# Grouped-query attention between two feed-forward layers: the matmuls for the row maxima take 128 contraction rows instead of 64, from a second, zero-padded copy of the keys

## The reference, cut to what matters

```python
x = x + 0.5 * ffn(layernorm(x), W_up, W_gate, W_down)
q, k, v = ...                                   # heads of width 16; k and v shared by 4 query heads
scores = einsum('bhqd,bhkd->bhqk', q, k) / sqrt(16)
scores = where(causal, -inf, scores)            # 256 x 256 for each of 16 x 16 (sequence, head)
x = x + softmax(scores) @ v
x = x + 0.5 * ffn(layernorm(x), W_up, W_gate, W_down)
```

## Time and profile before

| | us |
|---|---|
| median of 3 runs | 680.62 |
| lowest, highest | 678.63, 680.65 |
| span of the profiled execution (first to last instruction) | 676.7 |
| what lies around the span, if that execution took the median time | 3.9 |
| PE, DVE, ACT, POOL busy within the span | 612.5, 552.8, 361.8, 309.7 |

### The profile page before, as it was taken

The page is one execution under the profiler, slowest core; times in us unless marked ns, Lnnn a source line. Parts: engine busy times, 40 slices in busy tenths (PEclk is TensorE's granted clock), DMA queues, the critical chain, the costliest instruction groups (busy, mean ns, idle before and its releaser), DMA issues.

```text
span 676.7 us, 14252 instructions
## 1 busy us (share of the span) xinstructions
PE 612.5 (91%) x4276; PEld 339.8 (50%) x4276; DVE 552.8 (82%) x1964; ACT 361.8 (53%) x652; POOL 309.7 (46%) x288
## 2 busy tenths in 40 slices
PE   1768999999897899996999699998888999999998
PEld 1324555656465644543444345443444555555566
DVE  6999989899967869794888479795959999899964
ACT  3444444444443357673677557776775444444442
POOL 6876624343412236563474627473674344243400
PEclk9999999999998979997999989998999999999999
DMA  9411001110105131413050503131021231121201
GB/s 310 148 32 31 17 16 31 31 31 5 28 1 116 41 80 41 80 43 80 1 118 1 118 1 90 30 94 26 3 33 32 32 63 46 46 62 32 63 32 62
DMA packets 48342, 36.40 MB, mean 54 GB/s; under 512 B 33697, under 2 KB 44705, under 8 KB 47777
## 3 DMA queue, kind: packets, MB, share of 16 engines
q1 hardware_dynamic: 48288, 35.80, 22.9%
HBM read 18.22 MB, written 9.44 MB: 41 GB/s over the span
## 4 chain that ended last, share of the span: by engine, by line
PE 64%; DVE 16%; issue 7%; DMA 6%; ACT 3%; SPq 2%; POOL 1%; DVEq 1%; POOLq 0%; ACTq 0%
PE bank L1023 22%; PE bank L1035 12%; PE bank L1118 8%; PE bank L1145 7%; PE bank L1173 6%; DVE hl L740 5%; DMA k_st<-k_scratch 5%; PE bank L1182 4%; DVE hid L714 2%; DVE stats L645 2%; PE bank L1187 2%; PE bank L1196 1%; ACT silu L462 1%; ACT shared L539 1%; SPq L228 1%
## 5 line engine op out<-in xcount | busy, mean ns | idle before, releaser
L878 DVE CUSTOM_DVE_ANT_0 sm_out<-bank,mask 128x256 f16<-128x256 f32 (+1 forms) x512 | 157.7, 352 | 60.8 <-PE bank L1145 40.4
L462 ACT ACTIVATE silu<-bank,w_scale 128x512 f32<-128x512 f32 x128 | 87.8, 686 | 167.8 <-PE bank L1023 167.6
L539 ACT ACTIVATE shared<-bank,qk_scale 128x512 f32<-128x512 f32 x192 | 125.8, 682 | 65.1 <-PE bank L1173 63.6
L740 DVE TENSOR_TENSOR hl<-hid,hh 128x512 f16<-128x512 f32 x128 | 140.6, 1098 | 0.0
L1035 PE MATMUL bank<-wT_down,hh 128*128 128x256 f16 x512 | 118.8, 273 | 8.1 <-DVE hl L740 7.5
L1035 PE MATMUL bank<-wT_down,hl 128*128 128x256 f16 x512 | 118.7, 273 | 0.0
L714 DVE SCALAR_TENSOR_TENSOR hid<-silu,h_unit,bank 128x512 f32<-128x512 f32 x128 | 94.7, 740 | 28.2 <-ACT silu L462 24.8
L1023 PE MATMUL bank<-xh,wT_gate 128*128 128x512 f16 x256 | 98.1, 383 | 9.6 <-DVE hid L714 9.0
L1023 PE MATMUL bank<-xh,wT_up 128*128 128x512 f16 x256 | 98.3, 384 | 1.9 <-DVE xl L699 1.9
L1023 PE MATMUL bank<-xl,wT_up 128*128 128x512 f16 x256 | 98.3, 384 | 0.0
L1023 PE MATMUL bank<-xl,wT_gate 128*128 128x512 f16 x256 | 98.0, 383 | 0.0
(11 more groups left out here) (113 smaller groups left out, 831.3 us busy)
## 6 DMA issues: line engine op xcount, KB each, us to landing
q_st<-q_scratch SPq DMA_DIRECT2D x16, 512.0 KB, 5.8
q_scratch<-q_hl SPq DMA_DIRECT2D x8, 512.0 KB, 3.2
out_dram<-x SPq DMA_DIRECT2D x7, 512.0 KB, 2.9
x<-in_x_dram SPq DMA_DIRECT2D x1, 3072.0 KB, 15.1
k_st<-k_scratch SPq DMA_DIRECT2D x32, 64.0 KB, 6.1
x<-in_x_dram SPq DMA_DIRECT2D x2, 512.0 KB, 7.2
shared<-in_w_up_t_dram SPq DMA_DIRECT2D x2, 512.0 KB, 5.3
shared<-in_w_gate_t_dram SPq DMA_DIRECT2D x2, 512.0 KB, 7.6
```

Of the source, the lines that this page charges most:

```text
L462: act.activation(silu[:, e % 2, :], U[e % 2][:, :], ACT.Silu, scale=w_scale[:, 0:1]).then_inc(silu_ready, 1)
L539: act.activation(prob[:, place % 2, i, :], ST[(3 * place + i) % 2][:, :], ACT.Exp, scale=qk_scale[:, 4:5]).then_inc(exp_done, 1)
L740: dve.tensor_tensor(hl[:, par, e, :], hid[:, e % 4, :], hh[:, par, e, :], ALU.subtract).then_inc(hl_ready, 1)
L878: ins = dve.tensor_tensor_reduce(sm_out[:, i, cols], SM[i][:, cols], mask[:, S - size:S], 1.0, MASKED, ALU.add, ALU.max, rowmax[:, seq_par ...
```

## The change

The keys are stacked a second time, in `k_mx`, whose rows 64 to 127 are zero, and the matmuls for the maxima take all 128 rows of `q_st` and `k_mx`. The zero rows cancel whatever stands in rows 64 and 65 of `q_st`. Each read of a chunk has four DMAs of 64 KB more, each put ahead of one of the old four, and all ten are waited for. POOL clears the new rows once, early.

```diff
+        k_mx = sb("k_mx", [P, 2, G, TC], F16)
...
-        N_SCR, N_ST = 2, 6
+        N_SCR, N_ST = 2, 10
...
                     for twice in range(2):
                         rows = slice((2 * n + twice) * DH, (2 * n + twice + 1) * DH)
+                        sp.dma_start(k_mx[rows, par, :, :], k_scr[par, n]).then_inc(st_loaded[par], 16)
                         sp.dma_start(k_st[rows, par, :, :], k_scr[par, n]).then_inc(st_loaded[par], 16)
...
-            sp.wait_ge(const_ready, 3)
+            sp.wait_ge(const_ready, 4)
...
             pool.memset(q_st[64:P, :, :, :].bitcast(U32), 0).then_inc(const_ready, 1)
             pool.wait_ge(const_ready, 3)
+            pool.memset(k_mx[64:P, :, :, :].bitcast(U32), 0).then_inc(const_ready, 1)
+            pool.wait_ge(const_ready, 4)
...
-                                        q_st[0:4 * DH, par, HPG * g + j, rows:rows + P],
-                                        k_st[0:4 * DH, par, g, at:at + size],
+                                        q_st[:, par, HPG * g + j, rows:rows + P],
+                                        k_mx[:, par, g, at:at + size],
```

## The result

The kernel with the change takes 687.0 us, the median of 7 runs (683.68 to 691.93), against 680.62 us of 7 runs before (678.63 to 682.63). The ratio is 1.0092, with a 95% interval of 1.0051 to 1.0133, so it is slower by more than nothing. The forecast was 681 us, its range 672 to 689: that range holds the time. The forecast's own case, no difference that can be told (0.40, 677 to 685), didn't come; slower had been given 0.38.

The account below looks back on a forecast made before the run. PE was taken as the bound, losing 0.11 us per matmul-shape change, with DVE close behind and reads on the chain. 676.7 less 15.6 plus 9.9 (reads) plus 6.0 (clock) is 677.0; with 3.9 around it, 681 us, range 672 to 689.

Parts of the forecast that it names:

- PE's shape, passed by DVE: In the stretches between reads, removed 64/128-row changes at 0.11 us each, as far as DVE allows: 15.6 us saved.
- reads on the path, five of them: First read, three between loop ends and the last each land 1.5 us later: 7.5 us added.
- the second read: Wanted 11.1 us after its first issue, while the longer read takes 10.9: hidden, nothing added.
- DVE's stop at two loop ends: DVE loads code behind the read's packets; more data lengthens this 0 to 2 us, taken as 1.2 each, 2.4.
- the clock: Longer PE stops halve it after three reads, 1.5 us each, plus 0.75 each at first and last: 6.0 us.
- rival 1: DVE is no limit, so PE's whole saving counts, 22 us for 15.6: 674.5 us; chance 0.17.
- Rival 5: The extra transfers cost only 0.5 us a read: 675 us; chance 0.06.
- Rival 3: At both loop ends code packets wait behind the longer queue; DVE's stop grows 4 us, not 1.2: 688; chance 0.14.
- rival 7: Code packets get ahead of a read's second half; DVE's stop shrinks up to 7 us per loop end: 667; chance 0.03.
- rival 2: The clock stays up after the three reads, 4.5 us less than forecast: 676.5 us; chance 0.14.
- Rival 6: 128-row weight loads can't run ahead of matmuls on the same rows; 512 loads of 0.1 us exposed, tens slower; chance 0.01.
- POOL's clearing: POOL's early clearing of the new rows takes 1.7 us, hidden because POOL then idles 1.69 us.

Follow-up runs that it names:

- shape_only: The kernel before with the maxima's matmuls on 128 rows of its own stacks, no second copy and rows 64 and 65 not cancelled: 668.17 us, ratio 0.9784.
- before_again: The kernel before, unchanged, run and profiled a second time: 683.19 us, ratio 0.9996.
- narrow pair: narrow_before and narrow_shape: DVE's reductions cut to 16 columns of each head, with 64-row and 128-row maxima: 673.1 and 648.82 us.
- tiny_bytes: The changed kernel with the four new DMAs of each read cut to one eighth of their columns, all ten issues kept: 669.93 us, ratio 0.98.
- narrow_before: The kernel before with DVE's reductions cut to the first 16 columns of each head, maxima still on 64 rows: 673.1 us, ratio 0.9849.
- reads_only: The changed kernel reading and awaiting the second copy, but with the maxima still on 64 rows of k_st: 701.6 us, ratio 1.018.
- narrow_shape: The kernel before with DVE's reductions cut to 16 columns of each head and maxima on 128 rows, no second copy: 648.82 us, ratio 0.9511.
- filler: The changed kernel with twelve useless matmuls ahead of PE's wait at the three reads between loop ends: 681.58 us, ratio 0.9982 to the kernel before.

## Why the prediction was right and wrong

The sum by its own terms, beside what the profiles gave. The measured shape saving is the span of shape_only against before, 10.8 us, plus the 1.6 us of the first feed-forward; the other rows are after against shape_only. They sum to 4.3 us, and with those 1.6 to the 5.9 between the spans (682.6 less 676.7). These are single executions: against before_again's span (680.7) the first row would be some 4 us larger, and by the ratios the shape is 14.7 us and all the rest 21.0. The last row is what the other rows leave, the stretches between the reads.

| term | predicted, us | measured, us |
|---|---|---|
| PE's shape, passed by DVE | −15.6 | −12.4 |
| reads on the path, five of them | +7.5 | +12.0 |
| the second read | 0 | +2.2 |
| DVE's stop at two loop ends | +2.4 | −2.3 |
| the clock | +6.0 | +4.8 |
| sum | +0.3 | +4.3 |

**The shape.** Right in mechanism and price, and the 15.6 us lie within what the two profiles of before and the ratios allow (12.4 to 16.5): the spacing went from 0.32 to 0.22 us, and PE's busy time in a stretch with 25 changes fell by 2.8 us, 0.11 each. That DVE stops it halfway was right too (rival 1, DVE no limit, fell with the narrow pair), but I spread it wrongly. By stretch, shape_only against before, with what I took: between reads 0.7, 1.1 and 1.1 us (1.6 each), 236.9 to 271.4 3.0 (2.3), behind the loop ends 2.5 and 0.7 (2.2 each), the last 0.9 (3.0), the first none (1.1). These make about 10 (the second, the loop ends' and the last hold falls of the clock too); the rest of the 12.4 came at the loop ends' stops and inside the reads, where I had put nothing. The Trainium skill (TensorEngine Tiling (Array Packing), Key Properties) says that changing the tiling mode drains TensorE. The trace agrees in so far as a change costs 0.11 us, which is gone without it; the drain itself it doesn't show.

**A read's length.** The step "twenty per cent of 6.9 us" is mis-sized. I took the bytes as a share of the engines' busy time, and added 0.1 for the issues: 1.5. The rate over the whole read stays at 139 to 140 GB/s, so 20% more bytes take 20% of the read's 9.5 us, 1.9; with the rest it came to 2.2 on average against before, and to 2.4 against shape_only for the five (12.0 by 5). By tiny_bytes some 1.7 of the 2.2 is bytes and 0.5 the issues. Rival 5, transfers at 0.5 each, fell. That the trace's 139 GB/s "doesn't agree" with the ceiling of 435 GB/s that the prediction gives from the Trainium skill (DMA: Bandwidth & Descriptors, Specifications) was too strong: a rate below a ceiling agrees with it, and shows only that the ceiling isn't what sets this read.

**The second read.** This is the step that failed: "Of eight reads the second is hidden". I set 10.9 us of read against 11.1 us of cover, as if the cover stood still. The cover is PE's own work from the trigger to the first use. The windows of before and of after over it:

```profile
236.90:248.00 11.10, 11.10 (x70) 5.30 (x69) 6.91 (x48) 6.13 (x12) 2.97 (x6) 0.69 0.60 121
```

```profile
240.70:249.00 8.30, 7.69 (x69) 4.26 (x68) 6.68 (x46) 5.95 (x12) 2.96 (x5) 1.00 0.91 173
```

The same work is 11.1 us long at a granted clock of 0.69 and 8.3 us at 1.00. So the cover was in part the slow clock, which I hadn't looked up for this stretch, and in part the changes of matmul. The narrow pair parts the two, with a light DVE and the clock at 1.00 in both: the cover is 7.8 us with 64 rows and 6.9 with 128. So the changes are some 0.9 us of it (I counted 1.5 at the other reads), and at full clock the second read isn't hidden even without the change, in the window and the timeline of PE of narrow_before:

```profile
238.60:246.30 7.70, 7.70 (x68) 4.00 (x67) 3.68 (x40) 6.09 (x12) 2.97 (x6) 1.00 0.85 172
```

```profile
247.64 0.39 PE L1146 MATMUL bank<-k_st,q_st 64*128 64x256 f16 x2 [1.34 <-DMA k_st<-k_scratch]
```

With the cover at 8.3, even a read of the old length is waited for, 0.98 us in shape_only; with the longer one it is 3.20 in after:

```profile
252.18 0.39 PE L1149 MATMUL bank<-k_mx,q_st 128*128 128x256 f16 x2 [3.20 <-DMA k_st<-k_scratch]
```

In reads_only the clock is 0.69 here as in before, and PE doesn't wait. The difference of 2.2 us between after and shape_only is what the longer read costs at this place.

**The loop ends.** The sign was wrong: "More data lengthens this by 0 to 2 us" came out as 6.33 and 5.76 us for 7.79 and 8.19. Rival 3 fell and rival 7 is right in kind, at 2.3 us against shape_only (3.7 against before) where I allowed 14. That DVE stands for its code, which I took, fits all 24 loop ends; that more data delays the code doesn't. So this term helped, and the two longer reads there cost nothing.

**The clock.** Right in mechanism: behind stops of 3 us and more at the three reads it fell to 0.50, at 1.5 to 1.9 us each, and rival 2 fell. It fell behind the second read too, 2.1 us. The other stretches gave 2.2 us back, above all behind the second loop end and the last read, where the profile of shape_only had half clock for longer (10.2 and 6.8 us for 3.4 and 3.4); at the first and the last read I had put 0.75 each. That the stop of 3.5 us came near (2.98 and 3.22, with 4.75 at the third read) is luck: I added 1.5 for PE's earlier arrival, and in shape_only the three waits are 0.91, 0.94 and 0.47 us for 0.47, 0.44 and 0.63; and I added 1.5 for the landing, which took 1.9 to 3.4.

**The weight loads.** Rival 6 fell: a group's matmuls start 0.22 us apart with all loads on 128 rows. The Trainium skill (TensorE: Matmul & The Clock Gate, Part 3) has weight loads overlap only where the row group differs, and the trace disagrees.

**POOL's clearing.** Right; it takes 1.80 us where I took 1.7, and POOL still waits for its next step, in the timeline of POOL of after:

```profile
71.96 1.80 POOL L423 MEMSET k_mx<- 64x2048 uint32 x1
...
75.11 1.90 POOL L369 TENSOR_TENSOR xn<-x,mv 128x1024 f32<-128x1024 f32 x1 [1.35 <-DVE mv L659]
```

In one sentence: by this table the reads were 7 us dearer than I took, of which DVE's stop gave back 5 and the clock 1, and the shape saved what I took or up to 3 us less. The range held the time in part by luck, since these misses have opposite signs.

## What to carry to other kernels

A change of matmul shape costs 0.11 us here, and to remove it pays only as far as the next engine lets it: look at its idle time in each stretch, and take less than that. When an edit both shortens the work that covers a transfer and lengthens the transfer, work out the new cover, and look up the granted clock that the old one had, before calling the transfer hidden; and size a longer transfer by the rate over the whole read, not by its busy share. If padding must be zero, clear the few rows that aren't rather than copy the many that are: two 16 KB transfers did here what four of 64 KB did, and turned 6 us lost into 16 won.

## What the runs showed of the hardware

**With 64-row matmuls the clock mostly falls more, with PE busy.** Behind the last read the kernels whose maxima take 64 rows had half clock for 3.4 us (before) and 13.7 (before_again and narrow_before); reads_only had 27.3, but in an execution 20 us longer than its shortest. The eight with 128 rows never had more than 6.8 there (none in narrow_shape, 6.8 in shape_only and filler, 3.4 in the rest). A window of before_again:

```profile
465.00:471.00 6.00, 6.00 (x31) 1.73 (x30) 3.47 (x21) 3.41 (x7) 1.88 (x3) 0.50 0.01 1
```

PE is busy for all six microseconds, with 31 matmuls begun, where before begins 56 in the same window at 0.94. Behind the second trigger it is similar: the clock is 0.69 to 0.70 over some 11.1 us in before, before_again and reads_only, and 1.00 in narrow_before and in all eight with 128 rows. So part of what shape_only wins is the clock, not the changes of matmul: at that trigger 1.3 to 1.9 us (2.8, less 1.5 for 14 changes at 0.11 or the 0.9 of the narrow pair). PE's idle time ahead of the trigger doesn't tell them apart: before and after both have it, 0.58 us just ahead and 0.63 us two microseconds earlier. There is one profile of each, narrow_before has the lower clock at the one place and not at the other, and the cause wasn't tried; whether and why the shape matters to the clock stays open.

**DVE at the loop's end.** It restarts 2.0 to 2.3 us behind the end of the second packet of the instruction queue since the trigger, 24 times of 24, while that packet's end lies anywhere from 5.3 to 8.7 us behind the trigger.

**One read is longer than the rest.** The third, 12.87 us in after, 12.65 in filler and 12.29 in reads_only, against 10.88 to 11.68 for the others of after. One issue on SP takes 1.39, 1.45 and 1.88 us in it, where the others take 0.42; in before one pair of issues of the third read takes 1.20 us for 0.88. What it waits for wasn't tried.
